# A state-space block with a routed feed-forward layer: one sort of the tokens by pair of experts, and tiles of 128 tokens, in place of three sorts by expert

## What is computed

```python
def step(state, xb_t):
    state = tanh(state @ A.T + xb_t)
...
x2 = layernorm(x + layernorm(states @ C.T + D * x + x) * gamma + beta)
scores = sigmoid(x2 @ router_weight.T)
# the better of two groups of 4 experts, in it the best 2; weights are their scores, scaled to sum 1
g = einsum('th,ehi->tei', x2, w_gate); u = einsum('th,ehi->tei', x2, w_up)
y = einsum('tei,eih->teh', silu(g) * u, w_down)
shared = (silu(x2 @ sw_gate) * (x2 @ sw_up)) @ sw_down
out = layernorm(x2 + einsum('teh,te->th', y, comb) + shared)
```

## Time and profile before

| | us |
|---|---|
| median of 3 runs | 434.74 |
| lowest, highest | 433.67, 436.27 |
| the profiled execution | 432.89 |
| its span (first to last instruction) | 431.2 |
| PE busy, of the span | 290.8 (67%) |
| DVE busy | 228.2 (53%) |
| POOL busy | 182.0 (42%) |
| ACT busy | 146.0 (34%) |
| mean granted clock of PE | 0.877 of full speed |

### The profile page before, as it was taken

One profiled execution on the slowest core, in us unless ns is written; L12 is line 12 of the kernel. 1 busy time (PEld: TensorE's weight loads), 2 busy tenths in 40 slices (PEclk: granted clock), 3 DMA queues, 4 the chain that ended last, 5 costly groups with the idle time before them and its releaser, 6 DMA issues.

```text
span 431.2 us, 7523 instructions
## 1 busy us (share of the span) xinstructions
PE 290.8 (67%) x2167; PEld 233.1 (54%) x2167; DVE 228.2 (53%) x812; ACT 146.0 (34%) x320; POOL 182.0 (42%) x265
## 2 busy tenths in 40 slices
PE   6889998676509687837767495986888456766000
PEld 5889887564508566625545384764566234544000
DVE  2249936488698865688516522344542063634350
ACT  2544234453305251603632030435344024240111
POOL 2200121078671554553262406067620757716751
PEclk9999999996957998996988598799999869998555
DMA  5999400012125153742665277699999949932330
GB/s 196 326 334 406 186 0 2 0 63 86 62 85 100 36 135 102 182 125 84 145 184 137 100 193 144 152 199 223 306 224 209 201 115 244 269 137 88 106 97 30
DMA packets 87929, 64.84 MB, mean 150 GB/s; under 512 B 59976, under 2 KB 76112, under 8 KB 87888
## 3 DMA queue, kind: packets, MB, share of 16 engines
q1 hardware_dynamic: 81744, 47.54, 42.6%
q0 software_dynamic: 6144, 16.79, 12.8%
HBM read 16.86 MB, written 33.55 MB: 117 GB/s over the span
## 4 chain that ended last, share of the span: by engine, by line
PE 36%; DVE 19%; issue 14%; DMA 9%; POOL 7%; SPq 6%; ACT 5%; another core or an unknown queue 2%; POOLq 0%; ACTq 0%; DVEq 0%
PE bank L603 12%; PE bank L622 7%; POOL yback L1284 5%; PE bank L484 4%; DMA yback<-ys_dram,back_i 4%; PE bank L489 4%; DVE xskip L1096 3%; PE bank L525 2%; PE bank L522 2%; PE bank L537 2%; DMA xjob<-xs_dram 2%; SPq L358 2%; POOL rstd L1256 1%; DVE st L1100 1%
## 5 line engine op out<-in xcount | busy, mean ns | idle before, releaser
L622 PE MATMUL bank<-wd,h 128*128 (+1 forms) x276 | 80.4, 417 | 19.3 <-issue 10.4
L1284 POOL DMA_INDIRECT yback<-ys_dram,back_i x64 | 66.5, 1038 | 55.4 <-issue 32.9
L1269 POOL DMA_INDIRECT xs_dram<-xres,slot_i x64 | 65.4, 1022 | 40.5 <-DVE slot_i L982 21.3
L1074 DVE SCALAR_TENSOR_TENSOR h<-bank,u_un,sg 128x256 f32<-128x256 f32 x69 | 32.6, 474 | 75.3 <-ACT sg L749 59.4
L603 PE MATMUL bank<-xjob,wg 128*128 128x256 f16 x318 | 48.2, 291 | 34.5 <-DVE h L1074 23.5
L622 PEld LDWEIGHTS bank<-wd,h 128*128 128x128 f32 x276 | 51.1, 206 | 36.5 <-issue 30.5
L1252 POOL TENSOR_TENSOR rstd<-mv,eps 128x4 f32<-128x4 f32 (+1 forms) x32 | 7.5, 236 | 119.8 <-DVE mv L896 55.2
L603 PEld LDWEIGHTS bank<-xjob,wg 128*128 x318 | 29.1, 102 | 51.1 <-issue 45.2
L749 ACT ACTIVATE sg<-bank,g_un 128x256 f32<-128x256 f32 x69 | 32.5, 472 | 67.5 <-PE bank L603 58.5
L603 PE MATMUL bank<-xjob,wu 128*128 128x256 f16 x318 | 47.4, 289 | 0.0
L1096 DVE SCALAR_TENSOR_TENSOR xskip<-yback,gate,xskip 128x256 f32<-128x256 f32 x64 | 28.1, 481 | 28.8 <-DMA yback<-ys_dram,back_i 28.2
(11 more groups left out here) (170 smaller groups left out, 443.1 us busy)
## 6 DMA issues: line engine op xcount, KB each, us to landing
ys_dram<-wu SPq DMA_DIRECT2D x53, 256.0 KB
xs_dram<-zeros SPq DMA_DIRECT2D x3, 2048.0 KB, 12.9
out_dram<-xskip SPq DMA_DIRECT2D x16, 256.0 KB
xres<-in_L_attn_x_dram SPq DMA_DIRECT2D x7, 512.0 KB, 6.7
wd<-in_L_ffn_w_down_dram SPq DMA_DIRECT2D x1, 1024.0 KB, 9.2
xs_dram<-xres,slot_i POOLq DMA_INDIRECT x64
yback<-ys_dram,back_i POOLq DMA_INDIRECT x64
xjob<-xs_dram SPq DMA_TRANSPOSE x53
```

Of the source, the lines that this page charges most:

```text
L622: last = pe.matmul(ps_y[n % 2][:, t * DM:(t + 1) * DM], h[:, n % 3, t * P:(t + 1) * P], rhs, start=True, stop=True)
L1074: stt(h[:, n % 3, :], ps_gu[n % 2][:, SLOTS:2 * SLOTS], u_un[:, 0:1], sg[:, n % 2, :], ALU.mult, ALU.mult).then_inc(h_done, 1)
L1269: nc.gpsimd.indirect_dma_start(out=xs_dram[hp], out_offset=bass.IndirectOffsetOnAxis(ap=slot_i[:, t, r:r + 1], axis=0), in_=rows16[:, t, : ...
L1284: nc.gpsimd.indirect_dma_start(out=yback[:, u % 2, t, r, :], out_offset=None, in_=ys_dram[hp], in_offset=bass.IndirectOffsetOnAxis(ap=back ...
```

## The change

The tokens are sorted once, by pair of experts, into 12 regions of DRAM with room for all tokens each. A row now has 524 fp32 words: the two fp16 halves of x2, then x2 plus the shared expert's result in fp32, the eight gate weights and the number of the token (2,096 bytes). One indirect DMA per tile scatters it, 32 in all. Shared jobs all run in the periods, two in each, with one PSUM bank for `down`. With CHECKS = ((G - 1, L + 11),) there is one table, after the last group, for 43 tiles of 128 rows.

A tile of one pair is loaded as it lies (SP), transposed on PE, and up-projected for both experts with x2 as the stationary side and gate and up weights of one expert side by side as 256 moving columns; the product with the gate weight has tokens on partitions, is transposed on PE (fp32), and the two down projections add up in PSUM. The result is added to the row, normed, and sent to the output with one indirect DMA per tile (POOL). `combine`, `gather`, `back`, ys_dram, the transposing loads and the stores of results go. `choose` builds a code of the pair in place of two indices, and `weigh` works out the gates per group. In the code, for a tile j:

```diff
-    PARTS = ((0, 3), (3, 6), (6, 8))
-    SLOTS = 2 * P
-    JT = [TK * (g1 - g0) * GT // SLOTS + E - 1 for g0, g1 in PARTS]
+    CHECKS = ((G - 1, L + 11),)
+    NC = len(PAIRS)
+    CAP = L * P
+    W = 2 * DM + 12
...
+        def iterations(c):
+            j0, j1 = starts[c], starts[c + 1]
+            for i in range(j0, j1 + 8):
+                def of(name, lag):
+                    return [(name, i - lag)] if j0 <= i - lag < j1 else []
+                out = of("gp", 1) + of("u", 1) + of("us", 1) + of("uh", 1) + of("v", 2) + of("ve", 2) + of("t", 0) + of("te", 0)
+                out += of("d", 3) + of("dz", 3)
+                z, y = i - 3, i - 4
+                if j0 <= z < j1 and ENDS[end_of[z]][-1] == z:
+                    out.append(("rr", end_of[z]))
+                if j0 <= y < j1 and ENDS[end_of[y]][-1] == y:
+                    out += [("o", j) for j in ENDS[end_of[y]]] + [("os", j) for j in ENDS[end_of[y]]]
...
+            if p < G:
+                put(("A", p), ("M", p), ("r", p))
+            if g < G:
+                put(("Y", g, 0), ("T", g, 0), ("K", g, 0), ("Y", g, 1))
+            if 0 <= o < G:
+                put(("P", o), ("E", o))
+                put(*[("V", o, t) for t in range(T4)])
...
+            if g < G:
+                put(("T", g, 1), ("K", g, 1))
+                shared(2 * g)
+            if p < G:
+                put(("B", p), ("R", p))
+            if g < G:
+                put(("H", 2 * g), ("L", g), ("Q", g))
+                put(("W", 2 * g))
+                shared(2 * g + 1)
+                put(("D", g), ("H", 2 * g + 1), ("W", 2 * g + 1), ("Z", 2 * g))
...
-        xs_dram = [nc.dram_tensor(f"xs_dram{h}", (E * CAP[h] + SLOTS, 2 * DM), F16, kind="Internal").ap() for h in range(NP)]
-        ys_dram = [nc.dram_tensor(f"ys_dram{h}", (JT[h] * SLOTS, DM), F32, kind="Internal").ap() for h in range(NP)]
-        xres = sb("xres", [P, L, DM])
+        xs_dram = nc.dram_tensor("xs_dram", (NC * CAP + P, W), F32, kind="Internal").ap()
+        rows = sb("rows", [P, L, W])
+        xres, xskip = rows[:, :, 0:DM], rows[:, :, DM:2 * DM]
...
+            def load_tile(j):
+                if use_of(j):
+                    sp.wait_ge(out_sent[slot_of(j)], 16 * use_of(j))
+                row = sp.value_load(tabR[0:1, j:j + 1], min_val=0, max_val=NC * CAP)
+                sp.dma_start(trow(j), xs_dram[bass.ds(row, P), :]).then_inc(row_in[slot_of(j)], 16)
...
             def down(n):
                 pe.wait_ge(h_done, n + 1)
-                if n >= 2:
-                    if JOBS[n - 2][0] == "r":
-                        pe.wait_ge(y_kept, routed_upto(n - 2))
-                    else:
-                        pe.wait_ge(zbase_done, shared_upto(n - 2))
+                if n:
+                    pe.wait_ge(zbase_done, n)
...
+            def turn_tile(j):
+                pe.wait_ge(row_in[slot_of(j)], 16 * (use_of(j) + 1))
+                for a in range(2):
+                    for k in range(KT):
+                        last = pe.transpose(ps_tx(j)[:, a, k, :], row[:, a, k * P:(k + 1) * P], ident16[:, :])
+            def pair_of(j):
+                return [pe.value_load(tabE[0:1, r, j:j + 1], min_val=0, max_val=E - 1) for r in range(2)]
+            def up_tile(j):
+                pe.wait_ge(tx_kept, j + 1)
+                for r, e in enumerate(pair_of(j)):
+                    m = 0
+                    for k in range(KT):
+                        for pw, px in ((0, 0), (0, 1), (1, 0)):
+                            last = pe.matmul(ps_tu(j)[:, r, :, :].rearrange("p w i -> p (w i)"), xTt[:, j % 2, 2 * px + k, :],
+                                             w16[:, pw, bass.ds(e, 1), k, :, :].rearrange("p o w i -> p (o w i)"),
+                                             start=(m == 0), stop=(m == 3 * KT - 1))
+            def turn_h(j):
+                pe.wait_ge(th_ready, 2 * (j + 1))
+                for r in range(2):
+                    last = pe.transpose(ps_th(j)[:, r * P:(r + 1) * P], th_[:, j % 2, r, :], ident[:, :])
+            def down_tile(j):
+                pe.wait_ge(th_kept, j + 1)
+                for r, e in enumerate(pair_of(j)):
+                    last = pe.matmul(ps_ty(j), thT[:, j % 2, r, :], wd[:, bass.ds(e, 1), :].rearrange("p o d -> p (o d)"),
+                                     start=(r == 0), stop=(r == 1))
...
+            def keep_tile(j):
+                nc.scalar.activation(xTt[:, j % 2, :, :], ps_tx(j).rearrange("p a k t -> p (a k) t"), ACT.Copy).then_inc(tx_kept, 1)
+            def silu_tile(j):
+                nc.scalar.activation(tsg[:, j % 2, :, :], ps_tu(j)[:, :, 0, :], ACT.Silu, scale=g_un[:, 0:1]).then_inc(tsilu_done, 1)
+            def keep_h(j):
+                nc.scalar.activation(thT[:, j % 2, :, :], ps_th(j).rearrange("p (r t) -> p r t", r=2), ACT.Copy).then_inc(th_kept, 1)
...
+            for n in range(NC):
+                nc.vector.memset(codes[:, n:n + 1], float(sum(2 ** e for e in PAIRS[n])))
+                for r in range(2):
+                    nc.vector.memset(delta[:, 2 + r, n:n + 1], float(nexts[n][r] - PAIRS[n][r]))
...
+            def tile_inner(j):
+                for r in range(2):
+                    stt(th_[:, j % 2, r, :], ps_tu(j)[:, r, 1, :], tw[:, j % 4, r:r + 1], tsg[:, j % 2, r, :], ALU.mult, ALU.mult
+                        ).then_inc(th_ready, 1)
+            def tile_sum(j):
+                tt(z2, ps_ty(j), z2, ALU.add).then_inc(z2_done, 1)
+                nc.vector.bn_stats(st3[:, i % 2, t, :], z2).then_inc(st3_done, 1)
+                nc.vector.bn_aggr(mv3[:, i % 2, t, :], st3[:, i % 2, t, :]).then_inc(mv3_done, 1)
...
             def scatter(g, t):
-                for r in range(TK):
-                    nc.gpsimd.indirect_dma_start(out=xs_dram[hp], out_offset=bass.IndirectOffsetOnAxis(ap=slot_i[:, t, r:r + 1], axis=0),
+                nc.gpsimd.indirect_dma_start(out=xs_dram, out_offset=bass.IndirectOffsetOnAxis(ap=slot_i[:, l:l + 1], axis=0),
+                                             in_=rows[:, l, :], in_offset=None,
...
+            def send(j):
+                nc.gpsimd.indirect_dma_start(out=out_rows, out_offset=bass.IndirectOffsetOnAxis(ap=where[:, j:j + 1], axis=0),
+                                             in_=trow(j)[:, DM:2 * DM], in_offset=None,
```

More of the change, by code:

```diff
@@ new lines, in loads, with shared, period, some @@
+        def loads(c):
+            put(("N", c))
+            put(*[("ld", j) for j in range(starts[c], starts[c + 1])])
+        def shared(n):
+            put(("U", n), ("s", n))
+        def period(p, tiles=()):
+            g, o = p - 1, p - 2
+            tiles = list(tiles)
+            def some(k, of):
+                for it in tiles[len(tiles) * k // of:len(tiles) * (k + 1) // of]:
+                    put(*it)
+            if p < G:
+                put(("A", p), ("M", p), ("r", p))
[4 more added lines that the diff above has]
+                put(*[("V", o, t) for t in range(T4)])
+            some(0, 4)
@@ L102, in period @@
+            some(1, 4)
+            if g < G:
[3 more added lines that the diff above has]
+                put(("D", g), ("H", 2 * g + 1), ("W", 2 * g + 1), ("Z", 2 * g))
+            some(2, 4)
             if p < G:
                 put(("X", p, 0), ("X", p, 1))
-            put(("D", g))
-            jobs(*d)
-            if g in ends:
-                ranked(g)
-                put(*[("V", g, t) for t in range(T4)])
-                put(("N", part_of[g]))
@@ L124, in plan @@
-        period(7, r0[8:9], r0[9:10], r0[10:11], r0[11:12])
-        period(8, r0[12:13], r0[13:14], r0[14:15], r0[15:16])
-        jobs(*r0[16:], *shared(4), *shared(5))
-        halves = [(g0 * T4 // 2, g1 * T4 // 2) for g0, g1 in PARTS]
-        for h in range(1, NP):
-            u0, u1 = halves[h - 1]
-            u, n = u0, len(routed[h])
-            for j, what in enumerate(routed[h]):
-                jobs(what)
-                while u <= u1 and j >= 3 and (j - 3) * (u1 - u0) >= (u - u0) * (n - 4):
-                    combine(u, u0, u1)
-                    u += 1
-            while u <= u1:
-                combine(u, u0, u1)
-                u += 1
@@ L139, in plan @@
-        jobs(*shared(6), *shared(7))
-        for n in range(len(JOBS), len(JOBS) + LAG + 1):
-            put(("J", n))
-        for u in range(halves[-1][0], halves[-1][1] + 1):
-            combine(u, *halves[-1])
+            if g < G:
+                put(("Z", 2 * g + 1))
+            some(3, 4)
+        queue = []
+        for n in range(2):
+            shared(n)
+            put(("H", n), ("W", n), ("Z", n))
+        for p in range(2, G + 2):
+            take = queue[:len(queue) // (G + 2 - p)] if p < G + 1 else queue
+            queue = queue[len(take):]
+            period(p, take)
+            for c, (g, _) in enumerate(CHECKS):
+                if g == p - 2:
+                    loads(c)
+                    queue += list(iterations(c))
```

(12 more changed lines are left out.)

770 lines of the change are left out of this document (389 added, 381 removed), and 2 rows, old and new, of the table early.

## The result

The changed kernel takes 462.28 us (median of 4 runs, 460.74 to 466.31), the kernel before 434.21 us (427.35 to 436.27, 4 runs): ratio 1.075, 95% interval 1.057 to 1.093. It is slower by 28 us, where 458 us were forecast. Ratios and their intervals are worked out from the runs in the faster of two states in which this chip runs a kernel, medians from all runs, so the two can differ by up to a hundredth (in e1 and e12). The profiled execution took 460.74 us with a span of 459.0.

The account below looks back on a forecast made before the run. The routed stage was taken as bound by PE's instruction stream, the sorting stage as shared by PE and DVE. First tile at 239 us, plus 197 for tiles, 10 tail and 10 after: 456 span, 458 execution; range 425 to 485.

Parts of the forecast that it names:

- Scan end and serial jobs: Before the sort: 0.5 us added up to the second scan's end, then two shared jobs in series, 6.8 us.
- The period: Six sorting periods of 21 us: DVE's work 14.9, its waits, and PE restarting at perhaps half clock; 126 us in all.
- The last group and the table: From the sort's end at 214 to the first tile at 239: group 7, ranks, slots, table and first loads, 25 us.
- chain of 11 us: In the last group: transposes, logits, routing and two shared jobs, 11 us, ahead of 3 us for ranks and slots.
- the four scatters have landed by then: Ahead of the first tile: row scatters are done when the table's rows_known comes, about 7 us after the slots.
- The tile: 43 tiles at 4.6 us each, bounds 4.0 and 4.9, set by PE's instruction stream; 197 us to the last up projection.
- two extra loads: In each tile: four register loads where a job has two, adding 1.4 us at 0.7 each to the job's 2.7.
- 16 routed jobs now have to come after it: Routed stage: 16 routed jobs that ran inside the sort must run after it; no separate size given.
- The clock: Rival, chance 0.14: a third to a half of the tile stage runs at 1.2 GHz, 5.2 us per tile, 483 us.
- The tail: After the last up projection: last down projections, statistics, scales, final scaling and last send, 10.3 us, then 9.6 more.
- The array sets the pace: Rival, chance 0.13: register loads run ahead of the array, so a tile costs 2.9 to 3.0 us; 384 us.
- Records only: Rival, chance 0.11: loads cost only their records, 4.0 to 4.1 us per tile, periods of 20 us; 429 to 437 us.

Follow-up runs that it names:

- e1: Changed kernel with each tile's pair of expert numbers read once, behind the waits, and kept for the down projection; 452.61 us, ratio 1.068, 4.28 us per tile.
- e12: As e9, but the 13 tiles of the first table all run after the last period and use both product banks; 442.33 us, ratio 1.061.
- e6: As e1, with the two register loads ahead of the up projection's waits; 404.44 us, ratio 0.934, 3.13 us per tile.
- e8: Changed kernel with forty unused matmuls ahead of the first down projection of each sorting period; 461.26 us (one run).
- e2: Changed kernel with the pair read twice ahead of the up projection, six register loads per tile; 558.67 us (one run), 6.82 us per tile.
- e3: Changed kernel without register loads, each tile using fixed (wrong) experts; 388.18 us (one run), 2.81 us per tile.
- e9: Changed kernel with the loads of e6 and two tables, 13 tiles placed in the last two periods and 30 after; 437.77 us, ratio 1.011.
- e10: Changed kernel with its own four loads and two tables, 13 tiles placed in the last two periods; 492.02 us, ratio 1.141.
- e11: Kernel before, one register load per routed job as in e4, but ahead of the up projection's waits; 425.73 us, ratio 0.988.
- e4: Kernel before with the expert number read once per routed job, in up, and kept for down; 409.09 us, ratio 0.973.

## Why the prediction was right

The forecast mechanism held, and most terms of the sum with it. That the total came out within 5 us also took some luck: the last group was 4 us longer than forecast and the tail 1.5, and 3 us of it the shorter tile stage gave back (243.5 to 437.6, 194 us in place of 197).

*Scan end and serial jobs.* Forecast 81.6 and the sort at 88; measured 82.1 and 89.1 in the profiled execution (e6: 81.3 and 88.3).

*The period.* Forecast 21 us, six of them 126. Measured: five from 89.1 to 194.0, 21.0 each, and the sixth ends near 214.5. The size was right, and so was its reason. DVE's work (14.9 forecast, 14.2 busy) and its waits make it, and PE's restart at half clock adds to them: 21.5 against 19.1 us by the forecast, 21.5 against 19.3 in the first period of the changed kernel and of e8, which ran once. The restart is felt as DVE's wait of 2.00 us for the second shared job's silu. Of the other waits the projection's two are 2.05 us (2.5 forecast), the addition's 1.29 (0.9).

*The last group and the table.* Forecast 25 us after 214, the first tile at 239; measured 243.5, which is 29 us after 214.5. Two steps failed. The "chain of 11 us" up to ranks and slots took 15 (these begin at 229.6), and they themselves 1 us where 3 were put down, so that cost 2 us. And "the four scatters have landed by then" does not hold. The chain of waits in that stretch runs past the table:
```profile
231.59 0.20 DVE rows L1094
...
236.85 2.74 DMA xs_dram<-rows,slot_i
...
240.81 2.68 DMA xT<-xs_dram
```
The four scatters can't start before the gate weights are in their rows, start 1.3 to 1.7 us apart on POOL, and the last lands at 239.6; the table's rows were written by 238.1, so that costs 1.5 us. The landing of 3.1 us was right at 2.7.

*The tile.* Forecast 4.6 us, measured 4.46: four loads, "issue" as the main wait of up and down, as foretold. The price of 0.7 for a load was a little high: it is 0.64 from start to start in the sequencer's records. (The Trainium skill, Perfetto Trace Analysis, section "Sequencer-only Instruction (DRAIN, etc)", which the prediction weighed, says that such a record holds only the execution; this case's 0.47 us of records in 0.64 of time agree.) But "two extra loads" was too simple a model of the tile. By it e1 should have given 3.2 us and gave 4.28, since a sequencer that has less to do meets the next wait sooner. The model counted durations of one stream and not where its waits stand.

*The clock.* The rival (0.14) did not come true: with 119 us of work in 174 the granted clock was 1.00. Only the first three tiles (5.3, 5.5 and 4.8 us) ran partly at 1.2 GHz, after the 14 us without work. (The Trainium skill, TensorE: Matmul & The Clock Gate, section "A second HAM failure mode: psum-queue depth-cycling", tells of a kernel whose clock swings for small idle times between groups of matmuls. By that the clock would have swung here; the trace shows 1.00 with two idle times of 0.5 and 0.8 us in every tile, and shows it at 0.75 in e2, with 2.5 us.)

*The tail.* Forecast 10.3 us from the end of the last up projection to the end of the last send, and 9.6 after it. Measured 15.0 (437.6 to 452.6) and 6.4. The step that was mis-sized is "scales 1.4, the final scaling 0.6, the last send 1.1": it took the last tile's way alone. POOL's timeline shows its queue instead; the last statistics are ready at 444.7, from then on POOL still works off two tiles' scales and three sends, of which the last ends at 452.6:
```profile
444.44 0.97 POOL L1395 DMA_INDIRECT out_dram<-xT,where  x1 [0.30 <-issue]
445.43 0.21 POOL L1362 TENSOR_TENSOR rstd<-mv,eps 128x1 f32<-128x1 f32 x1
...
447.27 1.08 POOL L1395 DMA_INDIRECT out_dram<-xT,where  x1 [0.61 <-issue]
...
451.59 0.97 POOL L1395 DMA_INDIRECT out_dram<-xT,where  x1 [0.30 <-issue]
```

*The other rivals.* "The array sets the pace" (0.13, 384 us) is not what the changed kernel does, but its size was right: e3 has 2.81 us per tile and 388 us (one run, in a place where the kernel before took 420). "Records only" (4.0 to 4.1) is excluded by the 0.64. Two of the prediction's ranges don't come out of their own ends: tiles of 4.3 to 4.9 and periods of 115 to 135 give 434 to 480, not 438 to 478, and "records only" with periods of 20 us gives 427 to 431, not 429 to 437. The step "16 routed jobs now have to come after it" is true, but e9, e10 and e12 show that it isn't the loss: with these buffers, routed tiles beside the sort cost more than they fill.

So the 28 us are made up of 57 us lost to where and how often PE's sequencer loads the pair (4.46 - 3.13 = 1.33 us, 43 times), and 29 gained by the rest of the change. e6 agrees: on one chip it is 58 us below the changed kernel (462.89 to 404.44), and 28 below the kernel before (432.64).

## What to carry to other kernels

A value that an engine's own stream loads into a register costs what the stream loses (0.64 us here, in records of 0.47), so count them per unit of work and read each once. Then try the load ahead of the waits that its user has: in the changed kernel the same two loads cost 1.15 us per tile more behind the wait. It is no rule, since in the kernel before the load ahead of the waits (e11) was not better than behind them (e4). When an experiment takes work from a stream and the time stays, look at which wait that stream now reaches sooner. Before an experiment that adds work is read, look whether the added work is in the way itself: e8's average hid 2.2 us. Before work is moved into a gap, count the buffers it may use there, and what drains at the border.

## What the runs showed of the hardware that was not expected

- Forty filling matmuls took 4.53 us. Where they ended when the next work was ready, the period ran at a granted clock of 1.00 and took 19.3 us in place of 21.5; where they ended 1.7 us later, it took 20.5 in place of 20.6 at 0.92.
- The clock stayed full at 68% busy with idle times under 0.9 us, and in e1 with one of 1.43 us per tile; twelve matmuls fell back to 1.2 GHz (2.74 us) in every tile in e2, where one idle time per tile was 2.5 us, while the down projection right behind them ran at 2.4 GHz (1.08 us).
- A register load on PE's sequencer takes 0.30 or 0.31 us at the median in every kernel here. The longest of 172 was 0.49 us at a DMA share of 0.24, and 1.08 in the kernel before, whose share was 0.92 in its routed stretch; whether the DMA traffic is the cause is not shown.
